# Two transformer layers: the product with the values turned round, its normalisation moved to columns, and new orders of the queues

## The chip, the cores and the metric

The kernel runs on one core of a Trainium2 chip. The metric is the device time of one execution in microseconds. Everything is computed in f32. The engines are named as in the profile: PE is TensorE (PEld its weight loads), DVE is VectorE, ACT is ScalarE, POOL is GpSimd, SP is SyncE, which here only issues DMAs.

## The reference

The input x has 32 sequences of 64 tokens with 256 features. Four layers follow one another: an attention over channels (layer 0), two transformer layers of the same form (1 and 2), and a recurrent layer (3). The change touches the layers 1 and 2 alone:

```python
def attention(q, k, v, mask):          # 16 heads of 16 features
    scores = jnp.einsum('bhqd,bhkd->bhqk', q, k) / jnp.sqrt(jnp.float32(HD))
    scores = scores * mask - 10000.0 * (1.0 - mask)
    probs = jax.nn.softmax(scores, axis=-1)
    return jnp.einsum('bhqk,bhkd->bhqd', probs, v)
ln_out = layernorm(hidden_states, ln1_s, ln1_b)
q, k, v = jnp.split(ln_out @ w_qkv + b_qkv, 3, axis=-1)
x = hidden_states + merge_heads(attention(..., ltor_mask)) @ w_ao + b_ao
q = layernorm(x, ln2_s, ln2_b) @ w_q + b_q
k, v = jnp.split(encoder_states @ w_kv + b_kv, 2, axis=-1)
x = x + merge_heads(attention(..., cross_mask)) @ w_co + b_co
return x + gelu(layernorm(x, ln3_s, ln3_b) @ w1 + b1) @ w2 + b2
```

The softmax may be taken in parts: the exponentials multiplied with the values, and the result divided by their row sums. Both kernels do that.

## The kernel before

**Phases.** Phase A (layer 0) ends some 100 us from the span's start. Phase B does the layers 1 and 2, and phase C the recurrent layer; the last transformer MLP is done together with the head of phase C (last_mlp_first_head).

**Phase B.** The 2048 tokens are four groups of 512 (8 sequences). Layer and group together make a turn, so there are 8 turns: first_turn, a hardware loop with turn for n = 1 to 6, and last_turn. A group is four tiles of 128 tokens (two sequences); k = 0 to 3 are its tiles in the self-attention, k = 4 to 7 the same in the cross-attention. In a turn also run the MLP of the turn before (norm_T_mlp, hidden, mlp_out; not in the first) and the projections for the turn after (norm_T_in, queries_in, keys_in, values_in; not in the last). What runs in which order on an engine is written out by hand in the bodies of turn, first_turn and last_turn, once for each of PE, ACT, DVE and POOL. Each engine works its list strictly in order and waits on semaphores.

**One tile.** PE computes all 16 heads' scores (L1055). DVE multiplies by the mask (L1691) into sc, which holds two tiles; POOL adds the mask (L792); DVE takes the negative maximum of each row (L1698) and adds it (L1703); ACT takes the exponential in place (L1429). PE transposes the result in eight pieces (probs_T, L1065), ACT copies them to pT (L1434). Then comes the part that is changed. times_v (L1080) makes 16 products per tile: pT of a pair of heads and one sequence is the stationary side (128 rows, 64 queries), and the values of this pair, with a column of ones for each head (VW = 17, so 34 columns), are moved. The result has queries on the partitions, and in every 17th column the row sum. DVE takes the reciprocals (L1709) and multiplies them in (L1711) to c_tok; PE transposes c_tok twice (result_T, L1088); ACT copies to cT (copy_cT, L1439). PE projects (out_project, L1101), DVE adds the residual and takes statistics (L1720 to L1727), POOL takes the inverse deviation (L797), DVE normalises (L1732).

An f32 product is two instructions for each call in the trace. The shape before a form, as 128*64, is the part of the array that an instruction uses: rows and columns. Other shapes of use here: 32*64 for the scores (eight of them lie beside each other), 128*64 for the values' projection (project_v, L959), 128*128 for all else.

Of the kernel before, what the change touches and what calls it, by code (L numbers as in the profile page):

```python
# [34 lines left out]
VW = HD + 1  # L35
# [53 lines left out]
def build(nc, io):  # L89
    ctx = ExitStack()  # L90
    with ctx:
        def sb(name, *shape):
# [16 lines left out]
        sizes_b = {"self_q": (NC, GT), "self_k": (NC, GB, NM, S), "self_v": (GB, NPAIR, 2 * VW)}  # L109
# [5 lines left out]
                    "x_res": (NP, D), "cross_mul": (NP, S), "cross_add": (NP, S), "c_tok": (D,)}  # L115
# [76 lines left out]
N_ZERO = 6  # L192
# [4 lines left out]
def phase_a(nc, io, ps, w, x_mid, ld_b, ld_set, zero_ok, stored, b_loads, entry):  # L197
# [6 lines left out]
    with ctx:  # L204
# [110 lines left out]
        def _(pool):  # L315
# [9 lines left out]
            pool.wait_ge(zero_ok, 2)  # L325
            for a in ("self", "cross"):
                for odd in range(2):
                    pool.memset(w[a + "_v"][odd * S:(odd + 1) * S, :, :, odd * VW + HD:odd * VW + VW], 1.0).then_inc(zero_ok, 1)
# [251 lines left out]
def phase_b(nc, io, ps, w, x_mid, ld_b, ld_c, ld_set, zero_ok, a_stored, b_loads, entry, stored, c_loads, head):  # L580

    ctx = ExitStack()
    with ctx:
# [22 lines left out]
        inv_sum, c_tok = sb("inv_sum", NH), w["c_tok"]  # L606
# [17 lines left out]
        pT_ps, pT_ok, v_sum_ps, inv_ok, tok_ok, c_ps, c_ok = (sem(n) for n in ("pT_ps", "pT_ok", "v_sum_ps", "inv_ok", "tok_ok", "c_ps", "c_ok"))  # L624
# [19 lines left out]
        def tile(n, k):  # L644

            return TILES * n + k
# [13 lines left out]
        def _(sp):  # L660
# [89 lines left out]
            sp.wait_ge(v_sum_ps, tile(TURNS - 1, NP))  # L750
# [8 lines left out]
        def _(pool):  # L759
# [57 lines left out]
            def turn(n, prev, nxt, entry_of=None):  # L817

                next_add_mask(n, 0, nxt)
                add_bias(prev, 6)  # L820

                last_inv_std(n, 0, prev)
# [3 lines left out]
                add_bias(prev, 7)  # L826
# [3 lines left out]
                inv_std_in(nxt if entry_of is None else entry_of)  # L830
                add_bias(n, 0)
                add_bias_in(nxt, 0)

                last_inv_std(n, 3, prev)
                next_add_mask(n, 3, nxt)
                add_bias_in(nxt, 1)
                add_bias_in(nxt, 2)

                last_inv_std(n, 4, prev)
                next_add_mask(n, 4, nxt)  # L840
                next_add_mask(n, 5, nxt)
# [2865 lines left out]
```

## Time and profile before

| | |
|---|---|
| median of 3 runs | 1084.66 us (1083.53 to 1088.22) |
| the profiled execution | 1083.26 us, span 1081.4 us |
| PE busy | 1006.8 us, 93% of the span |
| PEld busy | 691.9 us, 64% |
| DVE busy | 764.7 us, 71% |
| ACT busy | 525.8 us, 49% |
| POOL busy | 434.1 us, 40% |
| granted TensorE clock, mean | 0.983 |
| DMA | 41.10 MB, mean 38 GB/s |

Busy is the time in which at least one instruction of the engine was under way. A matmul's record is much longer than the time for which it keeps the next one from starting (they are pipelined), so for PE the distance between starts says more than the busy share. A clock of 1.00 is 2.4 GHz. DMAs are of no weight in phase B.

### The profile page before, as it was taken

What the parts mean: (1) busy time and instruction counts of PE and PEld (TensorE: products, weight loads), DVE (VectorE), ACT (ScalarE), POOL (GpSimd) and SP (SyncE); (2) the same over time, 40 slices, a digit from 0 to 9 for tenths busy, and PEclk for the clock granted to TensorE, in tenths of its full rate; (3) what the DMA queues carried; (4) which work ended last, traced back from release to release, by engine and by line L of the source; (5) the groups of instructions that cost most, each with busy time, mean ns of one, the idle gap of its engine ahead of it and who ended that gap; (6) DMA issues with size and microseconds to landing.
All of it is one profiled execution on the core that took longest, in us unless ns stands there. A gap on an engine that the chain in (4) does not pass through costs nothing. (4 is left out here: it accounts for less than half of the span.)

```text
span 1081.4 us, 24322 instructions
## 1 busy us (share of the span) xinstructions
PE 1006.8 (93%) x9328; PEld 691.9 (64%) x9328; DVE 764.7 (71%) x1527; ACT 525.8 (49%) x1012; POOL 434.1 (40%) x387
## 2 busy tenths in 40 slices
PE   7997899999999999999999999998986998989967
PEld 5775667677677678778678678775463453553535
DVE  3784879766766766856756757854459798997965
ACT  4672464563663673573573582572421544525432
POOL 2122544533533443452442543441417517355260
PEclk9999899999999999999999999999998999999998
DMA  8230100000001002103000000210010001010010
GB/s 266 79 108 21 35 12 22 26 21 22 26 21 61 25 21 70 40 21 100 25 21 22 25 21 21 79 58 20 1 40 23 1 24 38 0 39 3 1 39 20
DMA packets 38003, 41.10 MB, mean 38 GB/s; under 512 B 8640, under 2 KB 33536, under 8 KB 37648
## 3 DMA queue, kind: packets, MB, share of 16 engines
q1 hardware_dynamic: 37776, 39.54, 11.4%
q8 instruction: 79, 1.29, 0.5%
q14 instruction: 20, 0.16, 0.1%
q0 software_dynamic: 128, 0.10, 0.0%
HBM read 31.25 MB, written 8.39 MB: 37 GB/s over the span
## 5 line engine op out<-in xcount | busy, mean ns | idle before, releaser
L792 POOL TENSOR_TENSOR head_area<-head_area,b_self_add 128x1024 f32<-128x1024 f32 x32 | 82.0, 2562 | 152.6 <-DVE head_area L1691 152.6
L792 POOL TENSOR_TENSOR head_area<-head_area 128x1024 f32<-128x1024 f32 x32 | 75.7, 2365 | 140.5 <-DVE head_area L1691 140.5
L2558 POOL TENSOR_TENSOR c_rs<-c_st,head_area 128x512 f32<-128x512 f32 x64 | 83.9, 1342 | 97.5 <-DVE c_st L3348 96.6
L1698 DVE TENSOR_REDUCE b_neg_max<-head_area 128x16 f32<-128x1024 f32 x64 | 77.9, 1217 | 40.8 <-POOL head_area L792 40.5
L1118 PE MATMUL ps<-b_hT_mlp,wl 128*128 128x512 f32 x224 | 105.3, 593 | 0.0
L1132 PE MATMUL ps<-w,b_act_g 128*128 128x256 f32 x448 | 102.7, 382 | 0.0
L1429 ACT ACTIVATE head_area<-head_area 128x1024 f32<-128x1024 f32 x64 | 68.0, 1062 | 53.6 <-DVE head_area L1703 53.5
L1132 PEld LDWEIGHTS ps<-w,b_act_g 128*128 128x128 f32 x448 | 83.0, 190 | 12.3 <-ACT b_act_g L1455 1.0
L1434 ACT ACTIVATE head_area<-ps 128x512 f32<-128x512 f32 x128 | 69.5, 596 | 39.7 <-PE ps L1065 39.2
L949 PE MATMUL ps<-head_area,wl 128*128 128x512 f32 x176 | 84.2, 602 | 0.6 <-ACT head_area L1394 0.6
L1703 DVE TENSOR_TENSOR head_area<-head_area,b_neg_max 128x1024 f32<-128x1024 f32 x64 | 80.2, 1253 | 1.0
L3348 DVE TENSOR_TENSOR_SCAN c_st<-head_area,ps 128x512 f32<-128x512 f32 x64 | 73.3, 1200 | 2.5 <-ACT ps L3051 2.4
L1065 PEld LDWEIGHTS ps<-ident,head_area 128*128 128x128 f32 x512 | 59.6, 141 | 19.6 <-issue 13.0
L1065 PE MATMUL ps<-ident,head_area 128*128 128x128 f32 x512 | 67.1, 274 | 4.8 <-DVE head_area L1691 2.7
L1101 PE MATMUL ps<-wl,b_cT 128*128 128x256 f32 x252 | 67.0, 388 | 3.7 <-issue 2.3
L797 POOL TENSOR_TENSOR b_rstd<-b_var,minus_half 128x1 f32<-128x1 f32 x63 | 36.1, 574 | 82.1 <-DVE b_var L1727 82.1
L959 PE MATMUL ps<-wl,head_area 128*64 128x128 f32 x1024 | 64.4, 280 | 0.0
L959 PEld LDWEIGHTS ps<-wl,head_area 128*64 128x64 f32 x1024 | 56.9, 140 | 6.2 <-issue 5.2
L1439 ACT ACTIVATE b_cT<-ps 128x256 f32<-128x256 f32 x64 | 24.6, 385 | 71.0 <-PE ps L1088 70.9
L1101 PEld LDWEIGHTS ps<-wl,b_cT 128*128 128x128 f32 x252 | 44.8, 190 | 21.6 <-issue 11.6
L1118 PEld LDWEIGHTS ps<-b_hT_mlp,wl 128*128 128x128 f32 x224 | 38.9, 190 | 27.9 <-issue 25.5
L1447 ACT ACTIVATE b_act_g<-ps,vl 128x512 f32<-128x512 f32 x56 | 38.5, 690 | 29.6 <-PE ps L1118 29.6
(294 smaller groups left out, 2133.3 us busy)
## 6 DMA issues: line engine op xcount, KB each, us to landing
head_area<-x_mid SPq DMA_DIRECT2D x9, 512.0 KB, 3.8
wl<-in_wl SPq DMA_DIRECT2D x4, 1024.0 KB, 6.4
head_area<-in_ctxT SPq DMA_DIRECT2D x8, 512.0 KB, 4.3
x_mid<-b_x_out SPq DMA_DIRECT2D x8, 512.0 KB, 3.3
area<-in_wc SPq DMA_DIRECT2D x1, 2336.0 KB, 8.2
a_x_in<-in_x SPq DMA_DIRECT2D x16, 128.0 KB, 2.6
a_y_in<-in_ctx SPq DMA_DIRECT2D x16, 128.0 KB, 3.1
w<-in_w SPq DMA_DIRECT2D x2, 1024.0 KB, 9.7
```

The source lines that it names most:

```text
L792: pool.tensor_tensor(t, t, m.unsqueeze(1).broadcast_to([P, NH, S]), ALU.add).then_inc(add_ok, 1)
L949: mm = pe.matmul(ps[:, YB + c, :], weight(name, k, first + c * P, first + (c + 1) * P), rhs[:, k, :], start=(k == 0), stop=(k == NC - 1))
L959: mm = pe.matmul(ps[odd * S:(odd + 1) * S, YB + half, b * P:(b + 1) * P], lhs[:, k, t:t + S], weight(name, k, odd * P, (odd + 1) * P), sta ...
L1065: mm = pe.transpose(ps[:, PT + half, i * P:(i + 1) * P], sc[:, k % 2, half, 2 * i:2 * i + 2, :].rearrange("q i k -> q (i k)"), w["ident"][ ...
L1101: mm = pe.matmul(ps[:, CO, OUT], cT[:, half, p * P:(p + 1) * P], weight(("ao", "co")[a], half), start=(half == 0), stop=(half == 1))
L1118: mm = pe.matmul(ps[:, YB + j % 2, :], weight("w1", k, j * P, (j + 1) * P), hT_mlp[:, k, :], start=(k == 0), stop=(k == NC - 1))
L1132: mm = pe.matmul(ps[:, YB + MLP_BANK[p], 0:D], act_g[:, j, p * P:(p + 1) * P], w["w2"][:, j, :], start=(j == 0), stop=(j == NJ - 1))
L1434: act.activation(pT[:, b, :, :].rearrange("k i q -> k (i q)"), ps[:, PT + b, :], ACT.Copy).then_inc(pT_ok, 1)
L1698: dve.tensor_reduce(neg_max[:, k % 2, :], t, AX, ALU.max, negate=True).then_inc(max_ok, 1)
L1703: dve.tensor_tensor(t, t, neg_max[:, k % 2, :].unsqueeze(2).broadcast_to([P, 2 * NPAIR, S]), ALU.add).then_inc(sub_ok, 1)
L2558: pool.tensor_tensor(rs[:, i % BUFS, :], st[:, i % 3, :], rF[:, i // RS, :], ALU.mult).then_inc(rs_ok, 1)
L3348: dve.tensor_tensor_scan(st[:, i % 3, :], decay[:, i // RS, :, :].rearrange("f b t -> f (b t)"), ps[:, VB[i % 4], :], 0.0, ALU.mult, ALU.a ...
```

## The change

1. The values lie in the stationary side without columns of ones: 32 columns for a pair of heads (PW = 32), zero where the head doesn't match. The exponentials are moved, 64 queries at a time, and each product goes to 32 partitions of the result, by the pair's place i in its half. The result has features on the partitions: it is already transposed, in the columns 0 to 255 of its bank.
2. The row sums come from DVE: row_sums reduces the exponentials in sc (128x1024 to 128x16) and takes the reciprocals. ACT widens them to 16 columns a head (widen, 128x256), PE transposes them twice (inv_T, into columns 256 to 511 of the same bank), ACT copies them (copy_inv). normalize on DVE multiplies the product by them straight into cT.
3. result_T, copy_cT, the column of ones with its four memsets, and c_tok go. SP's loads for phase C wait for inv_ps instead of v_sum_ps.
4. The order of all queues of PE, ACT, DVE and POOL is new in first_turn, turn and last_turn.

```diff
-VW = HD + 1
+PW = 2 * HD
...
-                    for i in range(NPAIR // 2):
-                        j = half * NPAIR // 2 + i
-                        for b in range(2):
-                            q = slice(b * S, (b + 1) * S)
-                            mm = pe.matmul(ps[q, CX, j * 2 * VW:(j + 1) * 2 * VW], pT[:, half, i, q], vP[a][:, 2 * p + b, j, :],
-                                           start=True, stop=True)
-                mm.then_inc(v_sum_ps, 1)
-
-            def result_T(n, k):
-                pe.wait_ge(tok_ok, tile(n, k) + 1)
+                    for b in range(2):
+                        q = slice(b * S, (b + 1) * S)
+                        for i in range(NPAIR // 2):
+                            pe.matmul(ps[i * PW:(i + 1) * PW, CX, half * P + b * S:half * P + (b + 1) * S], vP[a][:, 2 * p + b, half * NPAIR // 2 + i, :],
+                                           pT[:, half, i, q], start=True, stop=True)
+
+            def inv_T(n, k):
+                pe.wait_ge(wide_ok, tile(n, k) + 1)
+                after(pe, c_ok, tile(n, k))
                 for half in range(2):
                     f = slice(half * P, (half + 1) * P)
-                    mm = pe.transpose(ps[:, CX, f], c_tok[:, f], w["ident"][:, :])
-                mm.then_inc(c_ps, 1)
+                    mm = pe.transpose(ps[:, CX, D + half * P:D + (half + 1) * P], inv_wide[:, f], w["ident"][:, :])
+                mm.then_inc(inv_ps, 1)
...
-            def copy_cT(n, k):
-                p = k % NP
-                act.wait_ge(c_ps, tile(n, k) + 1)
-                act.activation(cT[:, :, p * P:(p + 1) * P], ps[:, CX, CT].rearrange("f (h q) -> f h q", h=2), ACT.Copy).then_inc(c_ok, 1)
+            def widen(n, k):
+                act.wait_ge(inv_ok, 2 * tile(n, k) + 2)
+                after(act, inv_ps, tile(n, k))
+                act.activation(inv_wide[:, :].rearrange("q (i d) -> q i d", d=HD), inv_sum[:, k % 2, :].unsqueeze(2).broadcast_to([P, NH, HD]), ACT.Copy).then_inc(wide_ok, 1)
+
+            def copy_inv(n, k):
+                act.wait_ge(inv_ps, tile(n, k) + 1)
+                after(act, c_ok, tile(n, k))
+                act.activation(inv_cols[:, :], ps[:, CX, D:2 * D], ACT.Copy).then_inc(cols_ok, 1)
...
+            def row_sums(n, k):
+                t = sc[:, k % 2, :, :, :].rearrange("q b i k -> q (b i) k")
+                dve.wait_ge(exp_ok, tile(n, k) + 1)
+                after(dve, wide_ok, tile(n, k) - 1)
+                dve.tensor_reduce(inv_sum[:, k % 2, :], t, AX, ALU.add).then_inc(inv_ok, 1)
+                dve.wait_ge(inv_ok, 2 * tile(n, k) + 1)
+                dve.reciprocal(inv_sum[:, k % 2, :], inv_sum[:, k % 2, :]).then_inc(inv_ok, 1)
+
             def normalize(n, k):
...
+                p = k % NP
+                dve.wait_ge(cols_ok, tile(n, k) + 1)
+                dve.tensor_tensor(cT[:, :, p * P:(p + 1) * P], ps[:, CX, CT].rearrange("f (h q) -> f h q", h=2),
+                                  inv_cols[:, :].rearrange("f (h q) -> f h q", h=2), ALU.mult).then_inc(c_ok, 1)
```

PE's new order in a turn of the loop is this (last_project k projects tile k - 1; last_project 0 the last tile of the turn before):

```
last_project 0, keys_ctx 0 | probs_T 0, keys_ctx 1, times_v 0, inv_T 0, scores 2, values_ctx 0 1, last_project 1
probs_T 1, norm_T_mlp, times_v 1, scores 3, hidden 0, norm_T_mid 0, inv_T 1, hidden 1, queries_mid 0, hidden 2
probs_T 2, last_project 2, hidden 3 4, times_v 2, scores 4, hidden 5, norm_T_mid 1, inv_T 2
probs_T 3, queries_mid 1, norm_T_in, last_project 3, queries_in 0, times_v 3, scores 5, queries_in 1, norm_T_mid 2, inv_T 3, keys_in 0
probs_T 4, queries_mid 2, times_v 4, last_project 4, scores 6, keys_in 1, hidden 6, norm_T_mid 3
probs_T 5, inv_T 4, queries_mid 3, hidden 7, times_v 5, scores 7, values_in 0
probs_T 6, inv_T 5, last_project 5, mlp_out 0, times_v 6, scores 0 of the next turn, mlp_out 1
probs_T 7, inv_T 6, last_project 6, values_in 1, times_v 7, scores 1 of the next turn, mlp_out 2, last_project 7, inv_T 7, mlp_out 3
```

DVE's new order in a turn of the loop (maximum, subtract and mask by the tile that they work on; 0' and 1' are of the next turn; residual and norm of 7p belong to the turn before):

```
row_sums 0, residual 7p, maximum 1, norm 7p, subtract 1, mask 2, normalize 0, values 0 1, residual 0, row_sums 1, norm 0
maximum 2, mask 3, cross_masks, subtract 2, normalize 1, stats_in, row_sums 2, residual 1
maximum 3, norm_in, subtract 3, norm 1, mask 4, row_sums 3, normalize 2
maximum 4, subtract 4, residual 2, norm 2, mask 5, row_sums 4, normalize 3
maximum 5, subtract 5, residual 3, mask 6, norm 3, row_sums 5
maximum 6, normalize 4, subtract 6, mask 7, values of the next turn 0
maximum 7, row_sums 6, normalize 5, subtract 7, mask 0', result 0, row_sums 7, residual 4, result 1
maximum 0', normalize 6, norm 4, subtract 0', residual 5, norm 5, values of the next turn 1, mask 1', result 2, normalize 7, residual 6, result 3, norm 6
```

## Rows read from the trace of the kernel before

**Rows 1.** The page, part 1: busy us, share of the span, instructions.
```profile
PE 1006.8 (93%) x9328; PEld 691.9 (64%) x9328; DVE 764.7 (71%) x1527; ACT 525.8 (49%) x1012; POOL 434.1 (40%) x387
```

**Rows 2.** Stretches: length, busy PE, PEld, DVE, ACT, POOL, PEclk, DMA share, GB/s.
```profile
102.00:171.27 69.27, 59.32 (x839) 44.16 (x820) 55.60 (x110) 33.22 (x60) 33.69 (x29) 0.95 0.06 19
...
254.19:338.39 84.20, 82.44 (x929) 61.22 (x929) 56.64 (x120) 45.03 (x74) 35.02 (x32) 1.00 0.12 36
...
420.96:503.32 82.36, 82.36 (x928) 61.22 (x929) 56.32 (x119) 45.02 (x74) 33.31 (x30) 1.00 0.09 27
...
669.16:742.00 72.84, 71.47 (x783) 54.18 (x782) 49.69 (x114) 38.84 (x65) 28.92 (x26) 1.00 0.19 65
```

**Rows 3.** Waits of DVE, 420.96 to 503.32: us in total, times, longest.
```profile
DVE b_x_cur L1720 <- PE ps L1101: 7.0, 4, 2.7
```

**Rows 4.** Order of time, PE from 441: start, length of the merged block.
```profile
442.46 1.04 PE L1065 MATMUL ps<-ident,head_area 128*128 128x128 f32 x8
443.33 1.88 PE L1118 MATMUL ps<-b_hT_mlp,wl 128*128 128x512 f32 x4
445.15 1.13 PE L1080 MATMUL ps<-area,head_area 128*64 128x34 f32 x32
446.20 0.69 PE L1055 MATMUL ps<-head_area 32*64 32x128 f32 x32
446.83 0.44 PE L979 MATMUL ps<-ident,b_xc 128*128 128x128 f32 x2
```

**Rows 5.** Order of time, PE from 475.
```profile
479.23 1.97 PE L959 MATMUL ps<-wl,head_area 128*64 128x128 f32 x32
481.03 1.07 PE L1080 MATMUL ps<-head_area 128*64 128x34 f32 x32
482.04 0.69 PE L1055 MATMUL ps<-area 32*64 32x128 f32 x32
...
491.62 1.04 PE L1065 MATMUL ps<-ident,head_area 128*128 128x128 f32 x8
492.58 1.97 PE L959 MATMUL ps<-wl,head_area 128*64 128x128 f32 x32
```

**Rows 6.** Order of time, PE from 819, in phase C.
```profile
820.12 1.07 PE L2746 MATMUL ps<-c_rs,area 128*32 128x512 f32 x8
821.11 1.08 PE L2741 MATMUL ps<-area,c_kv 128*128 128x128 f32 x6
```

**Rows 7.** Groups by line and form: count, busy us, mean ns, idle before.
```profile
L1080 PE MATMUL ps<-area,head_area 128*64 128x34 f32 x1024 | 36.4, 227 | 0.8 <-ACT head_area L1434 0.7
...
L1698 DVE TENSOR_REDUCE b_neg_max<-head_area 128x16 f32<-128x1024 f32 x64 | 77.9, 1217 | 40.8 <-POOL head_area L792 40.5
...
L1711 DVE TENSOR_TENSOR head_area<-ps,b_inv_sum 128x256 f32<-128x256 f32 x64 | 27.2, 425 | 2.2
...
L1709 DVE RECIPROCAL b_inv_sum<-ps 128x16 f32<-128x16 f32 x64 | 16.3, 254 | 38.3 <-PE ps L1080 38.0
...
L792 POOL TENSOR_TENSOR head_area<-head_area 128x1024 f32<-128x1024 f32 x32 | 75.7, 2365 | 140.5 <-DVE head_area L1691 140.5
...
L1429 ACT ACTIVATE head_area<-head_area 128x1024 f32<-128x1024 f32 x64 | 68.0, 1062 | 53.6 <-DVE head_area L1703 53.5
...
L1439 ACT ACTIVATE b_cT<-ps 128x256 f32<-128x256 f32 x64 | 24.6, 385 | 71.0 <-PE ps L1088 70.9
...
L447 ACT ACTIVATE a_x_keep<-a_x_in 128x256 f32<-128x256 f32 x16 | 6.7, 418 | 0.0
```

**Rows 8.** Order of time, PE from 101, in the first turn.
```profile
119.33 1.06 PE L1065 MATMUL ps<-ident,head_area 128*128 128x128 f32 x8 [2.09 <-ACT head_area L1429]
120.74 1.81 PE L1080 MATMUL ps<-area,head_area 128*64 128x34 f32 x32 [0.34 <-ACT head_area L1434]
```

**Rows 9.** Order of time, PE from 738: the end of the last turn.
```profile
738.59 0.38 PE L1088 MATMUL ps<-ident,head_area 128*128 128x128 f32 x2
740.09 1.10 PE L2071 MATMUL ps<-wl,b_cT 128*128 128x256 f32 x4 [1.11 <-PEq L1982]
```

More of the change, by code:

```diff
@@ L748, in _ @@
             store(5, rows[1])
-            sp.wait_ge(v_sum_ps, tile(TURNS - 1, NP))
+            sp.wait_ge(inv_ps, tile(TURNS - 1, NP))
             for dst, src in load_c_weights(w, io):
@@ L1208, in turn @@
                 next_scores(n, 5, nxt)
+                values_in(nxt, 0, prev)
+                probs_T(n, 6, nxt)
+                inv_T(n, 5)
                 last_project(n, 5, prev)
-                hidden(prev, 7, nxt)
-                probs_T(n, 6, nxt)
-                result_T(n, 5)
-                values_in(nxt, 0, prev)
+                mlp_out(prev, 0, nxt)
                 times_v(n, 6)
                 next_scores(n, 6, nxt)
-                mlp_out(prev, 0, nxt)
+                mlp_out(prev, 1, nxt)
@@ L1218, in turn @@
+                probs_T(n, 7, nxt)
+                inv_T(n, 6)
                 last_project(n, 6, prev)
-                result_T(n, 6)
-                mlp_out(prev, 1, nxt)
-                last_project(n, 7, prev)
-                probs_T(n, 7, nxt)
                 values_in(nxt, 1, prev)
@@ L1227, in turn @@
                 mlp_out(prev, 2, nxt)
[L1228 removed]
+                last_project(n, 7, prev)
+                inv_T(n, 7)
                 mlp_out(prev, 3, nxt)
@@ L1233, in first_turn @@
                 keys_ctx(n, 0, prev)
+                keys_ctx(n, 1, prev)
                 probs_T(n, 0, nxt)
-                keys_ctx(n, 1, prev)
+                times_v(n, 0)
+                inv_T(n, 0)
+                next_scores(n, 0, nxt)
+                values_ctx(n, 0)
+                last_project(n, 1, prev)
+                probs_T(n, 1, nxt)
+                norm_T_mid(n, 0)
+                times_v(n, 1)
+                values_ctx(n, 1)
+                next_scores(n, 1, nxt)
@@ new lines, in first_turn @@
+                next_scores(n, 5, nxt)
+                last_project(n, 5, prev)
+                keys_in(nxt, 1)
+                probs_T(n, 6, nxt)
+                times_v(n, 6)
+                next_scores(n, 6, nxt)
+                inv_T(n, 6)
+                last_project(n, 6, prev)
+                probs_T(n, 7, nxt)
+                values_in(nxt, 0, prev)
+                last_project(n, 7, prev)
+                times_v(n, 7)
+                inv_T(n, 7)
+                values_in(nxt, 1, prev)
@@ L1789, in turn @@
                 next_mask(n, 1, nxt)
+                cross_masks(n)
                 next_subtract(n, 1, nxt)
+                normalize(n, 1)
+                stats_in(nxt if entry_of is None else entry_of)
+                row_sums(n, 2)
                 last_residual(n, 2, prev)
                 next_maximum(n, 2, nxt)
+                norm_in(nxt if entry_of is None else entry_of)
+                next_subtract(n, 2, nxt)
                 last_norm(n, 2, prev)
-                next_subtract(n, 2, nxt)
+                next_mask(n, 2, nxt)
```

612 lines of the change are left out of this document (310 added, 302 removed).

## The prediction

> **What bounds the kernel now.** First the busy shares of the page: PE 93%, DVE 71%, ACT 49% [rows 1]. Then the busy time by stage. The two transformer layers run in eight turns; a turn begins where the output projection of the turn before is issued. The six turns of the loop last from 171.27 to 669.16, 82.98 us each, and the sample turn has PE busy 82.36 of 82.36 us at clock 1.00, DVE 56.32, ACT 45.02, POOL 33.31 [rows 2]. In the list of waits of that turn PE has no entry at all, while DVE's longest is one for PE [rows 3]. Busy PE alone could still hide gaps, so I read PE's instructions one after the other: every block starts where the one before has streamed its columns [rows 4, 5]. So a loop turn is a sum of PE blocks, and time taken from a block comes out of the turn as long as nobody else gets late. The last turn is alike (71.47 of 72.84). The first is not (59.32 of 69.27, clock 0.95 [rows 2]): there PE waits for the chain mask, add, maximum, subtract, exp [rows 8].
>
> **Part 1, values as the stationary side (L1080).** Now a tile's product is 32 instructions (16 calls, two passes) with 64 columns loaded and 34 moved, in two column groups. The block takes 1.05 us (445.15 to 446.20) [rows 4], 1.01 behind a block of its own shape [rows 5]: 8 tiles, 8.3 us a turn. What limits it? values_ctx/values_in load the same 64 columns and move 128, and take 1.80 us for as many instructions (479.23 to 481.03) [rows 5]. Moving 34 instead of 128 would need 1.80 x 34/128 = 0.48, so loads set the 1.05. They are halved to 32 columns, and 64 are moved. The moved side now sets: 1.80 x 64/128, halved again because four column groups instead of two work beside each other, 0.45. That four do is seen in phase c: eight instructions of 128*32 moving 512 columns stand in 0.99 us (820.12 to 821.11) [rows 6]; one behind the other at 1.80/16 us per 128 columns they would need 3.6. To the 0.45 comes what a block loses at its edges; the old block loses about 0.14, and I keep that: 0.59. Gain 8 x (1.04 - 0.59) = 3.6 us a turn. Bounds, since no row has this form: 0.50 (half of the 1.01) and 1.04 (no gain).
>
> **Part 2, changes of the array's shape.** A block of eight transposes takes 0.87 before another full-array block [rows 4] and 0.96 before one of another shape (491.62 to 492.58) [rows 5]: 0.10 a change. The old turn has 25 changes. The new one has 29, counted along the two lists: values_ctx and values_in had the product's shape and shared it at three places, and now don't, and in tiles 0 and 4 a full-array block stands between the product and the scores behind it. 4 x 0.10 = 0.4 us more. The bound upwards is a whole 0.2 each, 0.8; below, none.
> The Trainium skill (TensorEngine Tiling, Key Properties) says that changing the tiling mode drains the TensorE. If a drain meant waiting out the last instruction's whole mean of 0.227 us [rows 7], the term would be 0.9; the rows show 0.10, and they decide.
> Net of parts 1 and 2: 3.2 us a turn.
>
> **Part 3, transposes.** result_T (two transposes per tile) goes, inv_T (two) comes: the same PE time. But inv_T doesn't depend on the product. After times_v only one DVE multiplication is left before out_project, where reciprocal, multiplication, transposes and a copy stood. PE gains nothing in the loop, where it didn't wait; it gives the order some room.
>
> **Part 4, DVE.** Per tile comes a reduction over 128x1024, the form of the maximum, 1.22 us; the multiplication 128x256 from PSUM stays (0.43) and so does a reciprocal of 16 columns, now from SBUF instead of PSUM (0.25; I keep it) [rows 7]. +1.22 x 8 = 9.7 us a turn: DVE 56.3 to 66.0 of about 79, 83%. Its cover is its own idle time (26.0 us in the sample turn), but it works its queue in order. Behind each row_sums wait maximum or residual, which feed exp and the next normalisation; and row_sums itself waits for exp. I laid the new queues of PE, DVE, POOL and ACT beside each other, with 1.22 for mask, maximum, subtract and sum, 2.4 for POOL's add, 1.06 for exp [rows 7]. Nearly everywhere DVE delivers one to five us early. The tight place is tiles 2 and 3: stats_in, norm_in and cross_masks lie there too, exp of tile 3 ends some 0.4 us after PE could start probs_T, and normalize(2) some 0.3 after out_project could start. I take 0.7 us of new PE waiting a turn; bounds 0 and 3.2 (all the gain).
>
> **Part 5, ACT and POOL.** ACT gets widen: 128x256 from SBUF, 0.42, 8 times = 3.4 us; copy_inv is copy_cT's twin (0.385) [rows 7]. ACT goes from 45.0 to 48.4 of 79, and widen, unlike copy_cT, isn't on the way of the product; hidden. Without that cover it would cost those 3.4. POOL has the same additions and powers in a new order, 33.3 us of 79: nothing. The dropped ones in the value tiles are four tiny memsets before the turns: nothing. SP waits for inv_ps instead of v_sum_ps before phase c's weights, about the same moment, with no one waiting for it yet: nothing.
>
> **First turn.** PE stands still more than 10 us, so its 3.6 are no gain there. The chain counts. Its worst hole, 2.09 us of bare waiting for exp before the block at 119.33 [rows 8], came from the first product: keys_ctx(1) stood ahead of it, and mask(2) and subtract(1) stood in DVE's queue behind its normalisation. Now both keys_ctx come first, while PE waits anyway, and subtract(1) can run some 4 us earlier. Afterwards DVE (52 + 10 us) nearly fills the turn. I get 1 us less; bounds +4 and -4.
>
> **Last turn.** -3.6, +0.2 (two more changes), +0.5 for small waits. Its end gets worse: PE now waits 1.3 us between the last transposes and the next projection (738.59 to 740.09) [rows 9], with mlp_out between product and transposes. In the new order mlp_out goes ahead, times_v(7) follows probs_T(7) directly (in the first turn such a neighbour costs 0.5, 119.33 to 120.74 against 0.87 [rows 8]), and copy_inv and the multiplication lie bare: +0.9. Sum -2.0.
>
> **Sum.** 6 x (3.2 - 0.7) = 15.0, 1.0 and 2.0. One loop turn of 84.20 holds 1.5 us of waits that the others don't [rows 2]; a new order may or may not keep them, and I count half, 0.7. Together 18.7 us: 1083.26 of the profiled execution (span 1081.4 and 1.9 around it) becomes 1064.6. The median of the runs, 1084.66, is 1.4 higher, so I predict 1066.0. The cases below are told against the median too.
>
> **Rivals.**
> (a) The forecast, 1060 to 1073: 0.58.
> (b) No new waits, and the first turn's hole closes: 6 x 3.2 + 4 + 2.5 = 26, so 1059; the lower bound of a block (0.50 instead of 0.59, in 7 turns of 8 tiles) adds 5: 1054. For it: PE had no wait under the old order. Against: DVE is 10 us fuller. 0.13.
> (c) The block's price is one per instruction, not per column: 32 of them take 1.05 now, 0.033 each. Then nothing is gained and 29 changes, DVE's waits and the end remain: 6 x (0.4 + 0.7) + 1.6 in the last turn - 1.0 in the first = +7, 1092; with half of it true, 1080. Against: the scores' 32 instructions, eight groups wide, take 0.63, 0.020 each (446.20 to 446.83) [rows 4]. 0.09.
> The Trainium skill (TensorEngine Tiling, Instruction Overhead) gives each matmul some 60 cycles; at the 2.4 GHz of clock 1.00 that is 0.025 us, a block of 0.80 + 0.14, 0.8 us a turn gained before the 1.1 is paid, and a sum of about 1086. The scores' 0.020 speak against it here.
> (d) DVE's waits eat the gain: 2 to 3 us a turn instead of 0.7, 1073 to 1080. For it: 83% in one fixed order. 0.13.
> (e) Slower: DVE becomes the bound of a turn. Place: exp to row_sums to maximum of the next tile, so that masks, and with them POOL's 2.4 us, come late for every tile. A turn is DVE's 66.0 plus what it still idles; it idles 26.0 now [rows 2], waiting for PE and POOL [rows 3]. If more than 17.0 of it stays, the turn is longer than 82.98. With 20, 86.0 a turn, and 2 more in the first and in the last: 1084.7 + 6 x 3 + 4 = 1107. 0.07.
>
> **Chances.** Within 0.5% (5.4 us) counts as no change, which is about what a measurement of this kernel can tell. Faster: (a), (b), most of (d) and a little of (c), 0.81. Same: 0.10. Slower: (e) and the bad end of (c), 0.09. Range 1054 to 1080.
>
> **What would show it.** Right: PE busy still equal to the turn's length, turns of 79.5 to 80.5; the product's block near 0.59 from its start to the next block; DVE near 66 a turn; exp late for probs_T at one tile of a turn only. Part 1 wrong: blocks near 0.9 or more. Part 4 wrong: waits PE <- DVE or ACT of over 1 us a turn, at many tiles. Part 2 wrong: the block before a product of 128*32 stretched by more than 0.1.

## The result, and the profile after

| | before | after |
|---|---|---|
| median | 1085.14 us (1083.53 to 1088.22, 4 runs) | 1070.51 us (1069.47 to 1076.24, 4 runs) |
| ratio | | 0.9873, 95% interval 0.9831 to 0.9914 |
| profiled execution, span | 1083.26, 1081.4 us | 1070.31, 1068.5 us |

The changed kernel is 1.3% faster. 1066.0 was forecast, 1054 to 1080 its range.

The page, part 1, of after (busy us, share of the span, instructions), against [rows 1]:
```profile
PE 983.8 (92%) x9328; PEld 660.3 (62%) x9328; DVE 837.1 (78%) x1591; ACT 558.6 (52%) x1088; POOL 435.6 (41%) x383
```
PE has lost 23 us of busy time and DVE has gained 72; 64 sums of 1.21 us are 78. The span fell by 12.9 only, and PE is now busy for 92%, not 93. Of PE's 23, 4.2 lie in the first turn, where it stood still before too (busy 59.15 of 69.10 us there, now 54.96 of 68.89), and some came back as waiting in turn 1 and the last turn.

Stretches of after (length, busy PE, PEld, DVE, ACT, POOL, PEclk, DMA share, GB/s): first turn, loop turns 1, 2 and 4, last turn, against [rows 2]:
```profile
103.30:172.19 68.89, 54.96 (x829) 39.38 (x821) 63.54 (x116) 35.53 (x68) 33.37 (x27) 0.98 0.06 19
172.19:256.26 84.07, 81.11 (x936) 57.80 (x929) 70.58 (x133) 51.16 (x85) 38.44 (x33) 0.98 0.07 22
256.26:337.28 81.02, 79.28 (x928) 57.20 (x929) 66.16 (x130) 49.67 (x84) 33.92 (x29) 1.00 0.12 37
417.12:496.53 79.41, 79.27 (x928) 57.23 (x929) 64.53 (x127) 49.66 (x84) 33.92 (x29) 1.00 0.09 28
655.43:726.59 71.16, 67.56 (x777) 49.14 (x776) 60.27 (x121) 41.62 (x73) 26.33 (x25) 1.00 0.19 64
```
Turn 4 is what the forecast drew: PE busy for 79.27 of 79.41. Turn 1 is not: PE busy 81.11 of 84.07. In the last turn PE stands still for 3.6 us, and in the first DVE is busy for 63.54 of 68.89, so DVE, not PE, fills it.

Order of time of after, PE, loop turn 4 (start, length of the merged block), against [rows 4, 5]:
```profile
484.25 1.03 PE L1095 MATMUL ps<-wl,b_cT 128*128 128x256 f32 x4
485.20 1.97 PE L954 MATMUL ps<-wl,head_area 128*64 128x128 f32 x32
487.10 0.65 PE L1074 MATMUL ps<-head_area 128*32 128x64 f32 x32
487.69 0.69 PE L1050 MATMUL ps<-area 32*64 32x128 f32 x32
488.31 3.72 PE L1126 MATMUL ps<-w,b_act_g 128*128 128x256 f32 x16
```
The product (L1074) now takes 487.10 to 487.69, 0.59, where it took 1.01 between the same neighbours [rows 5]. The projection ahead of it (485.20 to 487.10, 1.90) is 1.80 plus one change of shape, 0.10.

That the gain is the product's, and not that of the new orders, can be read from loop turn 5 (503.32 to 586.02 before, 496.53 to 576.08 after), which has almost the same waits of PE in both (0.26 and 0.27 us). From start to start the eight products took 8.30 us and take 4.74; all other blocks together took 74.14 and take 74.54.

Groups by form in after (count, busy us, mean ns, idle before), against [rows 7]:
```profile
L788 POOL TENSOR_TENSOR head_area<-head_area,b_self_add 128x1024 f32<-128x1024 f32 x32 | 84.5, 2641 | 123.1 <-DVE head_area L1715 123.1
L1727 DVE TENSOR_TENSOR head_area<-head_area,b_neg_max 128x1024 f32<-128x1024 f32 x64 | 78.0, 1219 | 0.8
...
L1733 DVE TENSOR_REDUCE b_inv_sum<-head_area 128x16 f32<-128x1024 f32 x64 | 77.6, 1212 | 0.5 <-ACT head_area L1423 0.4
...
L1761 DVE TENSOR_SCALAR b_xc<-b_x_cur,b_mv,b_rstd 128x256 f32<-128x256 f32 x63 | 29.4, 468 | 8.4 <-POOL b_rstd L793 8.3
L1433 ACT ACTIVATE head_area<-b_inv_sum 128x256 f32<-128x256 f32 x64 | 26.9, 420 | 30.5 <-DVE b_inv_sum L1735 28.3 <-PE ps L1082 2.1
L1740 DVE TENSOR_TENSOR b_cT<-ps,head_area 128x256 f32<-128x256 f32 x64 | 26.8, 418 | 18.2 <-ACT head_area L1438 18.0
...
L1735 DVE RECIPROCAL b_inv_sum<-b_inv_sum 128x16 f32<-128x16 f32 x64 | 16.2, 253 | 2.2
```
Sum 1.21, reciprocal 0.25, widen 0.42, multiplication 0.42: the durations assumed. What doesn't fit is in the first line: POOL's addition with b_self_add has a mean of 2.64, and 2.4 was assumed for all. In before this group had a mean of 2.56 already (the 2.36 of [rows 7] is the other group's):
```profile
L792 POOL TENSOR_TENSOR head_area<-head_area,b_self_add 128x1024 f32<-128x1024 f32 x32 | 82.0, 2562 | 152.6 <-DVE head_area L1691 152.6
```
Seven of these 32 took 3.27 to 3.29 us there, one in the first turn and one in each loop turn; in after the one of each loop turn takes 3.68 to 3.69.

Where the 12.9 us came from, by stretches cut at PE's instructions (the six loop turns from 171.27 to 668.29 before and 172.19 to 655.43 after):

| stretch | before | after | difference | forecast |
|---|---|---|---|---|
| up to the first turn | 102.17 | 103.30 | +1.1 | 0 |
| first turn | 69.10 | 68.89 | -0.2 | -1.0 |
| loop turn 1 | 82.91 | 84.07 | +1.2 | -2.5 |
| loop turns 2 to 6 | 414.1 | 399.2 | -14.9 | -12.5 - 0.7 |
| last turn | 71.80 | 71.16 | -0.6 | -2.0 |
| behind it | 341.3 | 341.9 | +0.6 | 0 |

The five later loop turns gave 3.0 us each, more than the 2.5 forecast. Turn 1 gave nothing back and lost 1.2.

The list of waits of PE has one entry in loop turn 1 of after (us in total, times, longest):
```profile
PE ps L944 <- DVE area L1698: 2.5, 1, 2.5
```
All engines there in order of time:
```profile
173.03 1.22 DVE L1715 TENSOR_TENSOR head_area<-ps,b_self_mul 128x1024 f32<-128x1024 f32 x1
...
174.17 2.78 DVE L1761 TENSOR_SCALAR b_xc<-b_x_cur,b_mv,b_rstd 128x256 f32<-128x256 f32 x2
174.33 2.46 POOL L788 TENSOR_TENSOR head_area<-head_area,b_self_add 128x1024 f32<-128x1024 f32 x1 [2.94 <-DVE head_area L1715]
...
174.87 1.04 PE L1060 MATMUL ps<-ident,head_area 128*128 128x128 f32 x8
...
176.75 0.78 POOL L765 TENSOR_TENSOR head_area<-head_area,rl 128x256 f32<-128x256 f32 x1
176.86 0.68 DVE L1698 TENSOR_TENSOR area<-ps,rl 64x512 f32<-64x512 f32 x1
```
Two normalisations (L1761, 0.41 us each elsewhere) take 2.78 together. The second ends at 176.95, 0.16 behind the end of POOL's addition (174.33 + 2.46 = 176.79), and the values' copy that PE waits for (L1698) comes behind it. Before the experiments, the reading was: certain operations of DVE stand still while POOL's addition runs.

### The profile page after: what moved, and what is told of

It reads as the page before. It is cut to its first block and busy times, and to the rows that moved or that the text cites. A ratio compares the mean times of both kernels' runs of the same rounds, so it can differ in the third digit from the quotient of the medians.

```text
span 1068.5 us, 24715 instructions
## 1 busy us (share of the span) xinstructions
PE 983.8 (92%) x9328; PEld 660.3 (62%) x9328; DVE 837.1 (78%) x1591; ACT 558.6 (52%) x1088; POOL 435.6 (41%) x383
## 5 line engine op out<-in xcount | busy, mean ns | idle before, releaser
L788 POOL TENSOR_TENSOR head_area<-head_area,b_self_add 128x1024 f32<-128x1024 f32 x32 | 84.5, 2641 | 123.1 <-DVE head_area L1715 123.1
L2612 POOL TENSOR_TENSOR c_rs<-c_st,head_area 128x512 f32<-128x512 f32 x64 | 83.7, 1335 | 98.6 <-DVE c_st L3402 97.0
L1126 PEld LDWEIGHTS ps<-w,b_act_g 128*128 128x128 f32 x448 | 82.8, 190 | 13.8 <-issue 2.2
L944 PE MATMUL ps<-head_area,wl 128*128 128x512 f32 x176 | 85.1, 607 | 3.1 <-DVE area L1698 2.5
L1428 ACT ACTIVATE head_area<-ps 128x512 f32<-128x512 f32 x128 | 69.3, 599 | 33.4 <-PE ps L1060 33.3
L1722 DVE TENSOR_REDUCE b_neg_max<-head_area 128x16 f32<-128x1024 f32 x64 | 77.7, 1213 | 11.5 <-POOL head_area L788 10.8
L1727 DVE TENSOR_TENSOR head_area<-head_area,b_neg_max 128x1024 f32<-128x1024 f32 x64 | 78.0, 1219 | 0.8
L1733 DVE TENSOR_REDUCE b_inv_sum<-head_area 128x16 f32<-128x1024 f32 x64 | 77.6, 1212 | 0.5 <-ACT head_area L1423 0.4
L1438 ACT ACTIVATE head_area<-ps 128x256 f32<-128x256 f32 x64 | 24.4, 381 | 69.9 <-PE ps L1082 69.9
```

The costliest lines, as they stand in the source:

```text
L788: pool.tensor_tensor(t, t, m.unsqueeze(1).broadcast_to([P, NH, S]), ALU.add).then_inc(add_ok, 1)
L944: mm = pe.matmul(ps[:, YB + c, :], weight(name, k, first + c * P, first + (c + 1) * P), rhs[:, k, :], start=(k == 0), stop=(k == NC - 1))
L1126: mm = pe.matmul(ps[:, YB + MLP_BANK[p], 0:D], act_g[:, j, p * P:(p + 1) * P], w["w2"][:, j, :], start=(j == 0), stop=(j == NJ - 1))
L1722: dve.tensor_reduce(neg_max[:, k % 2, :], t, AX, ALU.max, negate=True).then_inc(max_ok, 1)
L1727: dve.tensor_tensor(t, t, neg_max[:, k % 2, :].unsqueeze(2).broadcast_to([P, 2 * NPAIR, S]), ALU.add).then_inc(sub_ok, 1)
L1733: dve.tensor_reduce(inv_sum[:, k % 2, :], t, AX, ALU.add).then_inc(inv_ok, 1)
```

## The experiments

Each kernel is the changed kernel with the edit shown; e7 starts from the kernel before. The ratios go by executions of before that were measured beside each kernel. "Turn 1" and "later turns" are lengths in the profiled execution; the later ones are the mean of the loop turns 2 to 6. The first turn is measured here from its first scores (75.7 us before, 75.4 after).

| | median us | ratio to before, 95% | first turn | turn 1 | later turns | last turn |
|---|---|---|---|---|---|---|
| before | 1085.14 | | 75.7 | 82.9 | 82.8 | 71.8 |
| after | 1070.51 | 0.9873 (0.9831 to 0.9914) | 75.4 | 84.1 | 79.8 | 71.2 |
| e1 | 1063.61 | 0.9796 (0.9761 to 0.9832) | 75.2 | 80.3 | 79.7 | 69.7 |
| e2 | 1066.66 | 0.9839 (0.9793 to 0.9885) | 73.3 | 83.0 | 80.3 | 70.2 |
| e3 | 1100.58 | 1.0148 (1.0101 to 1.0194) | 83.7 | 86.3 | 82.2 | 74.7 |
| e4 | 1062.64 | 0.9794 (0.9756 to 0.9832) | 75.0 | 80.6 | 79.6 | 70.1 |
| e5 | 1071.07 | 0.9885 (0.9843 to 0.9926) | 75.6 | 83.9 | 80.0 | 71.4 |
| e6 | 1092.33 | 1.0087 (1.0049 to 1.0126) | 75.4 | 85.3 | 83.1 | 74.1 |
| e7 | 1106.66 | 1.0229 (1.0182 to 1.0275) | 80.8 | 86.5 | 85.1 | 74.2 |
| e8 | 1062.75 | 0.9787 (0.9735 to 0.9839) | 71.6 | 82.3 | 79.7 | 70.2 |
| e9 | 1061.98 | 0.9776 (0.9739 to 0.9813) | 74.9 | 80.3 | 79.7 | 69.7 |
| e10 | 1066.85 | 0.9841 (0.9791 to 0.9890) | 77.9 | 80.7 | 79.9 | 71.2 |

**e1_ports.** Three moves in DVE's lists, so that operations which a running addition of POOL seemed to hold back don't stand behind the mask that starts it:
```diff
 first_turn, start:   -cross_masks(n)  row_sums(n, 0) ... next_maximum(n, 1)
                      +row_sums(n, 0) ... next_maximum(n, 1)  cross_masks(n)
 first_turn, end:     -next_mask(n, 7)  last_norm(n, 6)  last_norm(n, 7)
                      +last_norm(n, 6)  last_norm(n, 7)  next_mask(n, 7)
 last_turn:           -next_mask(n, 3)  last_norm(n, 3)  norm_in
                      +norm_in  next_mask(n, 3)  last_norm(n, 3)
```


> DVE's order alone is changed, at three places where a tensor_scalar of DVE starts just after POOL's 2.4 us addition and is recorded with 2.45 us instead of 0.3 to 0.4: cross_masks in the first turn go behind maximum(2), norm(5) and norm(6) go ahead of the next turn's first mask, norm_in in the last turn goes ahead of mask(5). Theory (a tensor_scalar waits until POOL's addition ends, and at these places PE waits for DVE): the three long records go, keys_ctx(1) of the second turn starts some 2 us earlier, and the time falls by 4 to 6 us, to 1065 to 1067. Rival (DVE is late there from its own 10 us of sums, the long records only fill time in which it would wait anyway): 0 to 2 us less, 1068.5 to 1070.5.

1063.61 us, 6.9 below after, somewhat more than the 4 to 6 expected. Turn 1 in e1 (columns as above):
```profile
170.83:251.09 80.26, 79.90 (x937) 57.12 (x929) 68.06 (x132) 50.94 (x85) 38.25 (x33) 1.00 0.08 23
```
It is 3.8 us shorter than in after, PE is busy for 79.90 of 80.26, and its wait has shrunk from 2.5 to 0.2. That is 2.3 of the 3.8. The rest is the clock: behind the wait of 2.5 the granted clock of after lay partly at 1.2 GHz. The same blocks of PE (keys_ctx(1), times_v(0), inv_T(0), scores of tile 2), first after, then e1:
```profile
178.38:183.43 5.05, 5.05 (x71) 2.40 (x71) 4.87 (x10) 2.25 (x4) 1.06 (x2) 0.66 0.34 104
```
```profile
174.97:178.46 3.49, 3.48 (x70) 1.82 (x71) 3.31 (x8) 3.05 (x7) 3.49 (x5) 1.00 0.13 22
```
They took 5.05 us at a clock of 0.66 and 3.49 at 1.00, so the held operation cost PE 1.6 us more than the wait shows. The last turn is 1.5 shorter: norm_in's first operation, held for 2.45 us beside POOL's addition in after, stood ahead of what ACT and the scores of tile 7 wait for; PE's wait of 1.0 there has gone to 0.2, and the next one of 0.7 is gone. The first turn, where one operation of cross_masks had been held for 2.47 us, gained only 0.2; DVE's 63 us fill that turn anyway.

**e10_handover.** The second of the three moves alone.
```diff
 first_turn, end:     -next_mask(n, 7)  last_norm(n, 6)  last_norm(n, 7)
                      +last_norm(n, 6)  last_norm(n, 7)  next_mask(n, 7)
```


> One of the three moves of e1 alone: at the end of first_turn DVE does its last two normalisations ahead of mask(nxt, 1) instead of behind it. Theory: the normalisation at the handover (2.46 instead of 0.41 us, beside POOL's addition) was what kept PE waiting 2.6 us in the turn after; that turn goes from 84.1 to about 80.3 and the time from 1070.5 to about 1066.7, more than half of e1's 7. Rival: DVE's backlog from the first turn is the reason (DVE busy 63.5 of 69 us there), and the wait only moves to the next tile: turn 1 stays over 83, 1069 to 1071.

1066.85, and turn 1 is 80.7: near the theory's 1066.7 and 80.3. So half of e1's gain is this one place. The profiled execution of e10 shows something else too: its first turn is 2.5 us longer than in after, with the same instructions. Stretches at the start of it, first after, then e10:
```profile
96.75:102.68 5.93, 5.93 (x97) 5.59 (x97) 2.74 (x5) 0.00 (x0) 2.36 (x1) 0.71 0.05 14
102.68:113.45 10.77, 7.22 (x116) 3.96 (x115) 10.19 (x11) 4.17 (x7) 5.14 (x5) 1.00 0.00 1
```
```profile
95.55:102.55 7.00, 7.00 (x96) 6.50 (x96) 2.74 (x5) 0.00 (x0) 2.36 (x1) 0.59 0.04 12
102.55:114.05 11.50, 7.95 (x117) 4.36 (x115) 10.53 (x11) 4.16 (x7) 5.15 (x5) 0.89 0.01 2
```
The granted clock is 0.59 and 0.89 where it was 0.71 and 1.00: more of it ran at 1.2 GHz instead of 2.4. It is a stretch in which PE is busy for only 7.2 of 10.8 and 8.0 of 11.5 us. One such execution says nothing of one or two microseconds in the first turn; the loop turns at 1.00 do.

**e2_light_sums.** What do DVE's sums cost? row_sums reduces a sixteenth, and its result isn't used.
```diff
-dve.tensor_reduce(inv_sum[:, k % 2, :], t, AX, ALU.add)
+dve.tensor_reduce(spare_sum[:, :], t[:, :, 0:4], AX, ALU.add)
```


> Part of the computation is left out: row_sums reduces 4 of the 64 columns, and the result isn't divided. DVE has about 1.1 us less to do per tile, all waits and the order stay. Theory (the reductions are hidden in the loop turns and bare in the first, in the handover to the second and at the end): loop turns 3 to 6 stay at 79.3 to 79.6, the first and second turn together lose 5 to 8 us, the last 1 to 2; 1060 to 1064. Rival (a fuller DVE costs something in each turn): the loop turns shorten too, by 0.5 us or more each; under 1060.

1066.66: a miss. DVE had 64 us less to do in sums and the kernel gained 4; the later loop turns even got 0.4 longer. The groups of e2 say why:
```profile
L1727 DVE TENSOR_TENSOR head_area<-head_area,b_neg_max 128x1024 f32<-128x1024 f32 x64 | 91.0, 1422 | 0.8
L788 POOL TENSOR_TENSOR head_area<-head_area,b_self_add 128x1024 f32<-128x1024 f32 x32 | 77.6, 2427 | 121.9 <-DVE head_area L1715 121.9
```
Now the subtraction has grown by 13 us and POOL's addition has shrunk by 7. The place, once a loop turn, is the same in both. All engines in order of time, after:
```profile
513.96 3.68 POOL L788 TENSOR_TENSOR head_area<-head_area,b_self_add 128x1024 f32<-128x1024 f32 x1 [3.38 <-DVE head_area L1715]
513.99 0.29 DVE L1707 TENSOR_SCALAR head_area<-head_area 128x256 f32<-128x256 f32 x1
514.20 1.22 DVE L1727 TENSOR_TENSOR head_area<-head_area,b_neg_max 128x1024 f32<-128x1024 f32 x1
```
and of e2:
```profile
510.54 2.55 POOL L788 TENSOR_TENSOR head_area<-head_area,b_self_add 128x1024 f32<-128x1024 f32 x1 [2.79 <-DVE head_area L1715]
510.57 0.29 DVE L1707 TENSOR_SCALAR head_area<-head_area 128x256 f32<-128x256 f32 x1
...
510.78 3.39 DVE L1727 TENSOR_TENSOR head_area<-head_area,b_neg_max 128x1024 f32<-128x1024 f32 x1
```
In after, DVE goes first and POOL's addition takes 3.68, which is 2.4 + 1.2; in e2 POOL goes first and the subtraction takes 3.39, about 1.2 + 2.2. They don't share, one of them waits the other out. The distances between the starts are alike (POOL's start lies 0.03 ahead of L1707 and 0.24 ahead of the subtraction in both), so these rows don't tell what decides who goes first. In e2 it went against DVE in all six loop turns, and the exponential behind came late:
```profile
PE ps L1060 <- ACT head_area L1423: 0.4, 1, 0.4
```

**e8_light_apart.** e2 again, with DVE's order changed so that this can't happen:
```diff
 turn:  -next_mask(n, 1)  cross_masks(n)  next_subtract(n, 1)
        +cross_masks(n)  next_subtract(n, 1)  next_mask(n, 1)
```


> e2_light_sums again (row_sums reduces 4 of 64 columns and its result isn't used, so the division is by 1), with one change of DVE's order in the turn of the loop: cross_masks and subtract(n, 1) run ahead of mask(3) instead of behind it, so that no operation of DVE that a running POOL addition could hold back lies beside that addition. Theory (e2 gained only 4 us because in each loop turn the subtraction, started 0.24 us behind POOL's addition, took 3.39 instead of 1.22 us, and the exponential behind it came late for PE): the subtraction takes 1.22 again, DVE's busy time falls by 13 us to about 775, PE's wait of 0.5 at that place goes, loop turns go from 80.0 to 79.4 or less, and the time from 1066.7 to about 1063. Rival (the steady turns of e2 are long for another reason, or mask(3), now 1.8 us later, makes the next exponential late by as much): turns of 80.0 or more, 1066 to 1068.

1062.75, as the theory said; DVE's busy time fell to 775.3 us, its subtraction to a mean of 1.219, and PE's wait at the exponential is gone:
```profile
L1727 DVE TENSOR_TENSOR head_area<-head_area,b_neg_max 128x1024 f32<-128x1024 f32 x64 | 78.0, 1219 | 0.8
...
L788 POOL TENSOR_TENSOR head_area<-head_area,b_self_add 128x1024 f32<-128x1024 f32 x32 | 76.6, 2394 | 129.6 <-DVE head_area L1715 129.6
```
The later turns (79.3 to 80.5, mean 79.7) came down by 0.6, a little less than said. So without its sums the changed kernel would gain up to 7.8 us: 3.9 in the first turn and 1.8 in turn 1, where DVE was the one that was late, but only 0.2 in each later turn. There the sums are nearly free. (The move itself gives nothing, as e9 shows below.)

The Trainium skill (SBUF — State Buffer, SBUF: two separate sides) describes this: VectorE and GpSimd share a pair of ports behind an exclusive lock, for VectorE operations in a two-port mode or with two inputs in SBUF, and the later one blocks. The traces agree on which operations suffer: tensor_scalar of 128x256 (0.41 becomes 2.46; in which mode it runs, no trace here shows) and the subtraction with both inputs in SBUF (1.22 becomes 3.39). In after, 20 of the sums and 24 of the multiplications with one input in PSUM (L1740) start while an addition runs, and none is longer than 1.22 and 0.43. On who blocks, the records don't bear the page out: in after POOL's addition starts first by them, by 0.24 ahead of the subtraction, and still it is POOL that waits, or its recorded start is not the moment that counts.

**e3_double_sums.** The full reduction twice a tile.
```diff
+dve.tensor_reduce(spare_sum[:, :], t, AX, ALU.add)
 dve.tensor_reduce(inv_sum[:, k % 2, :], t, AX, ALU.add)
```


> Each row_sums makes its reduction twice (the first goes to a spare tile): DVE 1.25 us more per tile, about 75 of 79.4 us in a loop turn. Theory (the sums are hidden as long as DVE keeps some room, and it has 14 us a turn, some of which it needs to wait for PE and POOL): loop turns grow by 1 to 3 us, the first by 6 to 10; 1085 to 1100. Rival (DVE was already the bound): each of the 64 reductions shows in full, +80, 1150. Rival (fully hidden in the loop): +8 to 12 in all, 1079 to 1083.

1100.58, 30.1 above after, just over the upper end of 1100. A loop turn of e3, and its two waits of PE:
```profile
514.34:596.18 81.84, 80.02 (x928) 57.12 (x929) 73.17 (x136) 49.74 (x84) 33.95 (x30) 1.00 0.16 48
```
```profile
PE ps L1112 <- ACT b_act_g L1446: 1.0, 1, 1.0
PE ps L1074 <- DVE b_cT L1741: 0.7, 1, 0.7
```
With 8.6 us more on DVE a turn grows by 2.4. The first wait lies at tile 2 of the self-attention, in the tight place of the prediction: widen comes late behind the two sums, and in ACT's queue the gelu that PE needs stands behind widen. The other, near the turn's end, is DVE's multiplication, late for the next product. The first sum is nearly free in a loop turn, the second costs 2.4: the order has about one sum's worth of room, and rival (e) starts close by. The first turn, already filled by DVE, pays 8.3 us at once.

**e7_before_sums.** The kernel before, in its old orders, with one unused reduction of 16 x 64 ahead of each reciprocal. It reads other data than the exponentials, so it waits for nothing new.
```diff
+dve.tensor_reduce(spare_sum[:, :], self_mul[:, :].unsqueeze(1).broadcast_to([P, NH, S]), AX, ALU.add)
```


> The kernel before, old orders, with one more reduction of 16 x 64 on DVE ahead of each reciprocal; its result isn't used. This is the DVE's part of the change alone. Theory (the old order has the room for it in the loop): loop turns grow by 0 to 1.5 us, the first by 4 to 8, the last by 1 to 3; 1092 to 1100. Rival (the sums are hidden only by the new order): +3 us or more in each loop turn, over 1108. Rival (hidden anywhere): within 3 us of 1085.

1106.66, 21.5 above before, above the theory's range and close to the rival. PE's longest entry among the waits from 170 to 756 us is
```profile
PE ps L1088 <- DVE head_area L1712: 14.4, 15, 1.1
```
In the old kernel result_T (L1088) stood behind DVE's reciprocal and multiplication, and a reduction ahead of them makes them late. Sums of the same size cost 21 us there and at most 8 (e8) in the new arrangement. How much of that the new orders do and how much the freed dependence of inv_T, this doesn't separate.

**e6_products_twice.** Every product twice.
```diff
-                    for b in range(2):
+                    for b in (0, 1, 0, 1):
```


> times_v issues each product twice. Theory (a loop turn is a sum of PE blocks, and the block costs 0.055 per round of four groups): 8 more rounds, +0.44 per tile, +3.5 a turn in the six loop turns and the last, less in the first: about 24 us more, 1092 to 1097. Rival (DVE now sets the turns): little more, under 1080. Rival (price per instruction as in the old block, 0.033): 32 x 0.033 = 1.05 per tile, +60.

1092.33, the theory. The block of 64 instructions and the next one:
```profile
437.77 1.10 PE L1074 MATMUL ps<-head_area,area 128*32 128x64 f32 x64
438.80 0.69 PE L1050 MATMUL ps<-area 32*64 32x128 f32 x32
```
1.03 for 64 against 0.59 for 32: 0.44 for the added 32, 0.014 each, and 0.14 at the edges. Both terms of the 0.59 (0.45 and 0.14) stand. What e6 doesn't separate is whether the 0.014 is a price of the 64 columns moved, as the prediction has it, or of an instruction: it excludes 0.033 and not 0.014. A loop turn grows by 3.3 of the 3.5 added (8 x 0.44): PE still sets it.

**e5_neighbours.** The loops over i and b exchanged, so that calls next to each other go to the same 32 columns of the array.
```diff
-for b in range(2):
-    for i in range(NPAIR // 2):
+for i in range(NPAIR // 2):
+    for b in range(2):
```


> The same 16 products per tile, but with the two sequences in the inner loop and the pair of heads outside, so that neighbouring calls go to the same column group. Theory (four groups work beside each other only when neighbouring calls use different ones): inside a group one follows the other at 0.055 us, only the borders overlap: (32 - 7) x 0.055 = 1.4 us a block instead of 0.49 from first to last start; with 8 blocks a turn PE gets 6 to 7 us longer a turn, about 1115. Rival (the order of the calls doesn't matter, since the passes are spread over the groups anyway, or the block's price is per instruction): blocks and time stay, 1070.

1071.07: my theory was wrong, and the rival right. The block and the next one:
```profile
444.72 0.69 PE L1074 MATMUL ps<-head_area,area 128*32 128x64 f32 x32
445.34 0.69 PE L1050 MATMUL ps<-head_area 32*64 32x128 f32 x32
```
0.62 instead of 0.59. The block stays nearly as short where neighbours in program order share a column group.

**e4_best.** e1, with the last projection of tile 3 behind the scores in the loop turn, and the end of the last turn in another order.
```diff
 turn, PE:       -last_project(n, 4)  next_scores(n, 4)
                 +next_scores(n, 4)  last_project(n, 4)
 last_turn, PE:  -last_project(n, 7)  probs_T(n, 7)
                 +probs_T(n, 7)  last_project(n, 7)
 last_turn, DVE: -result(prev, 3)  last_norm(n, 6)  last_norm(n, 7)  normalize(n, 7)
                 +normalize(n, 7)  result(prev, 3)  last_norm(n, 6)  last_norm(n, 7)
```


> The first kernel's three moves, and three more: out_project(3) goes behind the scores in the loop (one change of the array's shape less), out_project(6) goes between probs_T(7) and times_v(7) in the last turn, and DVE's normalize(7) goes ahead of the last result and norms. Theory (each change of shape costs 0.10, a product right behind probs_T waits 0.5): 6 x 0.1 + 0.5 + up to 0.9 less than the first kernel, so 1.5 to 2 us, 1063 to 1065.5. Rival: out_project(3) behind the scores makes normalize or residual late for norm_T_mid(3), and nothing or less is won.

1062.64, not to be told from e1. The last turn got 0.4 longer: the bare wait ahead of the first projection behind it went from 1.2 us in e1 to 2.2, and a wait of 0.3 ahead of the last product is gone.

**e9_apart_best.** e1, with the loop turn's move of e4 and the order of e8.


> A candidate for the best version: all of the changed kernel, with the three moves of e1_ports, last_project 4 behind the scores as in e4_best (loop turn only, not e4's changes of the last turn), and cross_masks and subtract(n, 1) ahead of mask(3) as in e8. Theory: POOL's addition of this tile takes 2.4 instead of 3.7 us in each loop turn, but starts 1.8 later, so tile 3 gets its exponential about 0.5 later than now, where DVE delivers early; loop turns 79.2 to 79.4, 1061.5 to 1063.5, against 1063.6 for e1. Rival: tile 3 is the tight tile (DVE has 65 of 79 us of work), the 0.5 comes through to PE in each turn: 1065 to 1067.

1061.98, ratio 0.9776 (0.9739 to 0.9813): the lowest median of all with the whole computation in it, and its interval lies apart from that of after. POOL's addition is back to 2.39, yet the later turns stay at 79.7 (79.2 to 79.4 expected): POOL had time for 3.7. Against e1 nothing measurable is gained.

## Why the prediction was right, and where it missed

The main case, (a), came true: faster, in its range of 1060 to 1073, but 4.5 us above the 1066.0 forecast. The profiled executions lie 12.9 apart, the medians 14.6, where 18.7 was forecast. The steady turns came out nearly as worked out; that the total stayed in the range owes something to a surplus there (2.4) which made up for part of what was lost at the places where stages meet.

- **Part 1, right.** 0.59 a block was forecast, 0.59 measured, and e6 confirms both halves of the sum. Only tile 4's block is longer in each loop turn, 0.79, with a bare 0.13 ahead of the projection that follows it. Rival (c), 0.033 an instruction, is out. By the Trainium skill's some 60 cycles for each matmul (TensorEngine Tiling, Instruction Overhead) the added instructions of e6 would take 0.025 us each at 2.4 GHz, an estimate from the page's figure; they took 0.014. That loads would be hidden held too. Four column groups at once, as read from [rows 6], held in either order of the calls.
- **Part 2, right.** A change of shape costs 0.10 with the new form too, and all blocks but the product take 0.40 more in loop turn 5, the 4 x 0.10 forecast. Parts 1 and 2 together: 3.56 - 0.40 = 3.16, and 3.2 was forecast.
- **Part 3, right in the loop:** nobody waits for inv_T in turn 4.
- **Part 4, somewhat too high in size, wrong in its list of mechanisms.** DVE rose from 56.3 to 64.5 a turn (66.0 forecast). In the loop turns 3 to 6 PE is idle for 0.1 to 0.6 us each, mean 0.3, against a mean of 0.1 in before: 0.2 of new waiting where 0.7 was taken, so the later turns gave 3.0 instead of 2.5. e3 shows that the margin was thin: rival (d) was one more sum away. What failed is the step "I laid the new queues beside each other, with 1.22 for mask, maximum, subtract and sum, 2.4 for POOL's add": durations on DVE and POOL are not independent of each other. A normalisation in the wrong place costs 2.46 instead of 0.41. PE waited 2.5 us for what stood behind it and then ran 1.6 us longer at the lower clock (e1), and that made turn 1 longer by 1.2 instead of shorter by 2.5: 3.7 us, the largest single miss.
- **Part 5, "POOL nothing", wrong in the same way.** POOL's time in a loop turn hardly rose (33.3 to 33.9), but its addition decided when DVE could work. The trace of before had the signs of it: one tensor_scalar of 2.47 us among its like of 0.28, beside POOL's addition, which lifts the mean of its group (L1683) to 0.56 where the like group L1682 has 0.29, and POOL's additions of 3.28. All engines of before in order of time:
```profile
114.30 0.28 DVE L1682 TENSOR_SCALAR head_area<-head_area 128x256 f32<-128x256 f32 x1
114.46 2.36 POOL L792 TENSOR_TENSOR head_area<-head_area,b_self_add 128x1024 f32<-128x1024 f32 x1 [2.47 <-DVE head_area L1691]
114.50 2.47 DVE L1683 TENSOR_SCALAR head_area<-head_area 128x256 f32<-128x256 f32 x1
...
116.89 1.21 DVE L1703 TENSOR_TENSOR head_area<-head_area,b_neg_max 128x1024 f32<-128x1024 f32 x1
```
- **First turn.** -0.2 against -1.0. The direction of the argument, DVE nearly fills it, is shown by e3 (+8.3) and e2 and e8 (-2.2 and -3.9). The 52 us of DVE in it stand in no row: [rows 2] have 55.60, and 63.54 were measured. The clock doesn't explain the missing 0.8: it was 0.95 in before and 0.98 in after, so it helped after. Its cause stays open.
- **Last turn.** -0.6 against -2.0. The end is as forecast (a bare wait of 1.2 between the last transposes and the next projection, 0.34 ahead of the last product), but norm_in, held beside POOL's addition, cost some 1.5 us around tile 7, which e1 gave back: the step of part 4 again.
- **The turn edge.** I had counted half of a wait of 1.5 us as gone. It stayed whole: turn 2 has 81.02 where its neighbours have about 79.5. 0.7 missed. The edge of 669.16 in the prediction lies one block late, since the last turn begins at 668.29: the old loop turns have a mean of 82.84, not 82.98, which changes none of the gains.
- **Outside the turns,** PE's same instructions took 1.7 us more in this execution. The first scores start at 95.6 to 97.9 us in the twelve traces, so a microsecond there says nothing of the change.

0.8 + 1.4 + 0.7 + 1.7 and, in the loop, 3.7 less the 2.4 that the later turns gave above the forecast: 5.9, the distance from 18.7 to 12.9 but for rounding. e1 and e10 show the part that could be had: with the three moves the time is 1063.6, 2.4 below the forecast.

**What stays open:** who goes first when DVE and POOL ask within some 0.2 us (after and e2 differ at equal distances); whether the product's 0.014 is a price of columns or of instructions; what the first turn kept of its 1.0; whether the old kernel's orders or its dependence of result_T on DVE made sums so dear there.

## What to carry to other kernels

Where one engine is busy all the time in a steady stage, price a change by the distances between its blocks in the trace; such a sum held to some 0.5 us a turn here. Then look at the places where stages meet: 3.7 us were lost at one handover, and a wait of PE there can cost more than its length, since the granted clock fell behind it. And before work is added to VectorE beside GpSimd, list the pairs that will run at the same time: tensor_scalar, or an operation with two inputs in SBUF, is best put ahead of what starts GpSimd's long operation, not behind it.

## What the runs showed of the hardware that was not expected

- Some operations of VectorE and GpSimd's addition exclude each other, operation by operation. A tensor_scalar of 0.41 us takes 2.46 beside an addition of 2.4, a subtraction of 1.22 takes 3.39, or GpSimd's addition takes 3.68 instead of 2.4. Which of them waits can turn over when nothing but DVE's load elsewhere changed (after against e2).
- 128*32 products that move 64 columns follow each other at 0.014 us an instruction over four column groups, whatever the order of the calls (0.62 against 0.59 a block).
- A wait of PE of 2.5 us in a steady stage was followed by a stretch at 0.66 of the clock, in which 3.49 us of work took 5.05 (after against e1, where a wait of 0.2 was followed by 1.00).
- The granted clock at the start of the first turn, behind a wait of PE of 2.4 us, differs from execution to execution (0.71 in after, 0.59 in e10 for the same instructions), and with what followed the first turn of e10 took 2.5 us longer.
